# Context attention in the first loop of a fused decoder: values with channels on partitions, denominators from a ones pattern, inverses spread by TensorE

## What is computed

```python
# linear attention, 8 heads of 32
q = x @ Wq + bq; k = x @ Wk + bk; v = x @ Wv + bv
Q = elu(q) + 1; K = elu(k) + 1
KV = einsum('nshd,nshv->nhdv', K, v / L)
Z = 1 / (einsum('nlhd,nhd->nlh', Q, K.sum(axis=1)) + EPS)
x = layernorm(x + einsum('nlhd,nhdv,nlh->nlhv', Q, KV, Z) * L)

# context attention, 16 heads of 16, 64 keys
q = (x @ Wq.T + bq); k = (ctx @ Wk.T + bk); v = (ctx @ Wv.T + bv)
scores = einsum('bqhd,bkhd->bhqk', q, k) / sqrt(16)
attn = softmax(scores)
out = einsum('bhqk,bkhd->bqhd', attn, v)
x = layernorm(x + out @ Wo.T + bo)
```

## Time and profile before

| | before |
|---|---|
| median of three runs | 1464.83 us (1463.44 to 1469.69) |
| profiled execution | 1464.9 us, span 1463.1 us |
| TensorE busy | 88% of the span |
| VectorE busy | 71% |
| ScalarE busy | 35% |
| GpSimd busy | 19% |
| TensorE on the chain that ended last | 75% of the span |
| last normalized rows of loop one | 398.2 us into the span |

### The profile page before, as it was taken

How to read it: one execution, slowest core, us unless ns; L and a number is a source line. 1 busy time by engine, 2 the same in 40 slices (tenths; PEclk the granted TensorE clock), 3 DMA queues, 4 the chain that set the end, 5 groups by cost and what they waited for, 6 DMA issues and landing times.

```text
span 1463.1 us, 17935 instructions
## 1 busy us (share of the span) xinstructions
PE 1287.1 (88%) x7132; PEld 877.9 (60%) x7132; DVE 1037.6 (71%) x1974; ACT 517.5 (35%) x602; POOL 277.1 (19%) x188
## 2 busy tenths in 40 slices
PE   7899999997789999856467999999999999998964
PEld 4566777765644454323345586776867686766653
DVE  4678888885344579967635487887879797878684
ACT  2333333332224567677211233222332323241310
POOL 0111111111000000027100041413223041414141
PEclk9999999996689999978688999999999999999997
DMA  4000000000152045499431202111111000000000
GB/s 191 15 15 30 30 29 15 30 15 0 58 217 101 29 152 192 131 327 325 153 110 41 92 3 68 42 55 55 51 48 62 30 22 19 27 24 28 0 15 15
DMA packets 47059, 104.66 MB, mean 72 GB/s; under 512 B 10496, under 2 KB 31104, under 8 KB 43648
## 3 DMA queue, kind: packets, MB, share of 16 engines
q1 hardware_dynamic: 42816, 101.42, 19.7%
q10 hardware_dynamic: 4160, 2.10, 0.5%
HBM read 59.47 MB, written 44.04 MB: 71 GB/s over the span
## 4 chain that ended last, share of the span: by engine, by line
PE 75%; DVE 13%; ACT 6%; issue 3%; DMA 1%; POOL 1%; SPq 0%; POOLq 0%; DVEq 0%; ACTq 0%
PE ps L1147 7%; PE ps L1207 7%; PE ps L1036 6%; PE ps L872 6%; PE ps L923 5%; PE ps L809 5%; PE ps L716 4%; PE ps L1180 3%; PE ps L1094 2%; PE ps L825 2%; PE ps L789 2%; PE ps L1118 2%; PE ps L1129 2%; PE ps L1224 2%; PE ps L1027 2%
## 5 line engine op out<-in xcount | busy, mean ns | idle before, releaser
L1207 PE MATMUL ps<-arena 128*128 128x256 f32 x512 | 119.8, 388 | 6.7 <-ACT arena L1603 6.7
L1630 POOL TENSOR_TENSOR arena<-arena 128x4 f32<-128x4 f32 x48 | 49.2, 1025 | 369.8 <-DVE arena L1790 369.8
L1147 PE MATMUL ps<-arena 128*128 128x512 f32 x256 | 117.6, 598 | 0.0
L1207 PEld LDWEIGHTS ps<-arena 128*128 128x128 f32 x512 | 98.4, 194 | 28.0 <-ACT arena L1603 10.2
L1036 PE MATMUL ps<-arena 128*128 128x256 f32 x384 | 89.5, 393 | 22.4 <-DVE arena L2051 20.2
L2096 DVE TENSOR_TENSOR arena<-ps,arena 128x2048 f32<-128x2048 f32 x32 | 73.3, 2292 | 39.4 <-PE ps L1094 39.1
L1694 POOL TENSOR_TENSOR arena<-arena 128x16 f32<-128x16 f32 x32 | 92.1, 2913 | 34.1 <-DVE arena L2125 34.1
L1036 PEld LDWEIGHTS ps<-arena 128*128 128x128 f32 x384 | 75.0, 198 | 33.7 <-issue 20.6
L872 PE MATMUL ps<-arena 128*128 128x512 f32 x192 | 85.3, 601 | 1.2 <-ACT arena L1322 1.2
L923 PE MATMUL ps<-arena 128*128 128x512 f32 x192 | 85.0, 595 | 1.4 <-ACT arena L1348 1.4
L809 PEld LDWEIGHTS ps<-arena 128*128 128x128 f32 x512 | 66.4, 209 | 17.9 <-ACT arena L1295 15.3
(11 more groups left out here) (246 smaller groups left out, 2649.9 us busy)
## 6 DMA issues: line engine op xcount, KB each, us to landing
v_scratch<-arena SPq DMA_DIRECT2D x7, 1536.0 KB, 8.5
arena<-v_scratch SPq DMA_DIRECT2D x7, 1536.0 KB, 6.7
up_scratch<-arena SPq DMA_DIRECT2D x6, 1536.0 KB, 7.3
arena<-up_scratch SPq DMA_DIRECT2D x6, 1536.0 KB, 9.4
arena<-x_scratch SPq DMA_DIRECT2D x16, 512.0 KB, 3.9
vw_scratch<-arena SPq DMA_DIRECT2D x32, 256.0 KB, 4.7
arena<-vw_scratch SPq DMA_DIRECT2D x8, 1024.0 KB
arena<-x SPq DMA_DIRECT2D x8, 512.0 KB, 4.2
```

The costliest lines, as they stand in the source:

```text
L1147: last = mm(flat(p % 2), w["cos_wq"][:, k, p * P:(p + 1) * P], xt4[:, k], start=k == 0, stop=k == NC - 1)
L1207: last = mm(flat(2)[:, C:2 * C], cos_pt[:, p], cos_vw[:, par, p], start=p == 0, stop=p == NP - 1)
L1630: g.tensor_tensor(var[0], var[1], neghalf[:, 0:NT], ALU.pow)\
```

## The change

The probabilities of a whole batch are kept: `xat_pt` has room for four tiles. For the values the sides are swapped: the block of values of a pair of heads (128 keys by 32 channels, without ones) is the weights, and the probabilities of that pair for all 512 rows are the moving side, eight products a batch, into four strips of 32 partitions of banks 6 and 7 (`xat_values`). The output thus lies with channels on partitions, as the projection wants it, so the turning of the output and its copy go. The sums come from `xat_denominators`: 32 products with a table of ones and zeros (`sums`, 46 columns, of which a window of 32 slides with tile and pair) as weights, which lay all sums of a batch on 128 partitions by 128 columns of bank 3. One reciprocal inverts them (`xat_reciprocals`). `xat_spread` multiplies the inverses by a second table (`spread`, 2x4x128 columns), so that each channel's partition gets its head's inverse, for all rows, in banks 0 and 1; ScalarE copies that (`xat_copy_spread`), and VectorE multiplies values by it once a batch (`xat_scale`). The output projection goes to banks 2 and 3. The order of the steps on every engine is new, and with it what each step waits for. The two packs that are read only at the start share room with `xat_pt`.

```diff
-            ("blk32", (P,))]
+            ("blk32", (P,)), ("sums", (46,)), ("spread", (NC, NT, P))]
...
-        vbd = ar.take(B, NP, 2 * HD + 2)
+        vbd = ar.take(B, NP, 2 * HD)
...
-        xat_pt = ar.take(NP, P)
-        xat_rec = ar.take(H)
-        xat_o = ar.take(NT, C)
+        probs_at = ar.at
+        xat_pt = ar.take(NT, NP, P)
+        probs_end = ar.at
+        xat_inv = ar.take(P)
+        xat_bc = ar.take(NC, T)
...
-            def xat_values(t):
...
-            def xat_turn_o(b, par):
...
+            def pair_at(c, j):
+
+                return j // 2 * 4 + c * 2 + j % 2
+
+            def xat_denominators(b, par):
+                wait(pe, "xat_probs_copied", b, NT, NT)
+                wait_ahead(pe, "lin_q_biased", b, 2, 1, 1)
+                wait_ahead(pe, "lin_scaled", b, 1, 2, 4)
+                wait_behind(pe, "xat_out_added", b, 1, 1, 1)
+                for t in range(NT):
+                    for c in range(NC):
+                        at = 14 - 4 * t - 2 * c
+                        for j in range(4):
+                            last = mm(flat(3)[32 * j:32 * j + 32, 0:P], w["sums"][:, at:at + 32],
+                                      xat_pt[:, t, pair_at(c, j)], start=t == c == 0,
+                                      stop=t == NT - 1 and c == NC - 1, skip_group_check=True)
+                last.then_inc(sig("xat_den_done").sem, 1)
+
+            def xat_values(b, par):
+                wait(pe, "xat_probs_copied", b, NT, NT)
...
+                for c in range(NC):
+                    for j in range(4):
+                        last = mm(flat(6 + c)[32 * j:32 * j + 32].rearrange("p (t n) -> p t n", t=NT),
+                                  vbd[:, b.off, 4 * c + j], xat_pt[:, :, pair_at(c, j)], start=True, stop=True)
+                last.then_inc(sig("xat_weighted").sem, 1)
+
+            def xat_spread(b, par):
+                wait(pe, "xat_inverted", b)
...
                 for c in range(NC):
                     for t in range(NT):
+                        last = mm(flat(c)[:, t * P:(t + 1) * P], w["spread"][:, c, t], xat_inv, start=True, stop=True)
+                last.then_inc(sig("xat_spread_done").sem, 1)
...
             unrolled(pe, [
...
+                (2, lin_out(1)), (2, lin_out(2)), (3, xat_turn_probs(2)), (2, lin_out(3)), (1, lin_project_kv(0)),
+                (1, lin_project_kv(1)), (1, lin_project_q(0)), (1, lin_project_q(1)), (3, xat_turn_probs(3)),
+                (1, lin_project_kv(2)), (3, xat_denominators), (2, lin_turn_y), (1, lin_project_kv(3)),
+                (2, xat_project_q), (3, xat_spread), (2, xat_scores(0)), (3, xat_values), (2, xat_scores(1)),
+                (3, xat_project_o), (2, xat_turn_probs(0)), (0, lin_turn_x), (2, xat_scores(2)), (1, lin_state),
+                (2, xat_turn_probs(1)), (2, xat_scores(3)), (1, lin_out(0))])
...
             unrolled(act, [
...
+                (3, xat_copy_probs(2)), (3, xat_exp(3)), (1, lin_bias_q), (3, xat_copy_probs(3)), (2, lin_copy_y),
+                (1, lin_exp_k), (2, xat_bias_q), (1, lin_exp_q), (3, xat_copy_spread), (2, xat_exp(0)),
+                (0, lin_copy_x), (2, xat_exp(1)), (2, xat_copy_probs(0)), (2, xat_copy_probs(1)), (2, xat_exp(2))])
...
             unrolled(pool, [
-                (3, rstd("xat", (xat_rs, xat_rs))), (2, xat_residual), (1, lin_add),
-                (1, rstd("lin", (lin_rs, lin_rs)))])
+                (0, lin_add), (0, rstd("lin", (lin_rs, lin_rs))), (2, rstd("xat", (xat_rs, xat_rs))),
+                (1, xat_residual)])
...
+            def xat_reciprocals(b, par):
+                wait(dve, "xat_den_done", b)
+                wait_previous(dve, "xat_spread_done", b)
+                v.reciprocal(xat_inv, flat(3)[:, 0:P]).then_inc(sig("xat_inverted").sem, 1)
+
+            def xat_scale(b, par):
+                wait(dve, "xat_weighted", b)
+                wait(dve, "xat_spread_copied", b)
+                wait_previous(dve, "xat_out_projected", b)
+                v.tensor_tensor(xat_ot.rearrange("p a b -> p (a b)"), flat(6, 2),
+                                xat_bc.rearrange("p a b -> p (a b)"), ALU.mult)\
+                    .then_inc(sig("xat_o_copied").sem, 1)
...
             unrolled(dve, [
...
+                (2, xat_shift(3)), (1, lin_stats), (0, lin_bias_kv(0)), (0, lin_bias_kv(1)), (1, lin_finish),
+                (3, xat_finish), (0, lin_bias_kv(2)), (0, lin_q_negative), (2, xat_reciprocals),
+                (0, lin_bias_kv(3)), (0, lin_k_negative), (2, quantize_part), (0, lin_k_features),
+                (1, xat_shift(0)), (2, xat_scale), (0, lin_q_features), (1, xat_shift(1)), (2, xat_add),
+                (1, xat_shift(2)), (0, lin_mask_state), (3, xat_peak), (0, lin_scale(0)), (0, lin_scale(1)),
+                (0, lin_scale(2)), (0, lin_scale(3))])
```

More of the change, by code:

```diff
@@ L268, in decoder @@
         w.update(w4)
[L269 to L271 removed]
+        assert ar.at <= probs_end
         ar.at = weights
@@ L735, in step @@
                         wait(pe, "lin_q_ready", b)
-                        wait_next(pe, "lin_x_copied", b)
-                    if LIN_BANKS[t] == 3 and not b.first():
-                        pe.wait_ge(sig("xat_normed", NT).sem, sig("xat_normed", NT).at(b, -1))
+                    if t == 0:
+                        wait_ahead(pe, "lin_x_copied", b, 1, 1, 1)
+                        wait_behind(pe, "xat_spread_copied", b, 2, 1, 1)
+                    if t == 1:
+                        wait(pe, "lin_q_biased", b)
+                        wait_behind(pe, "xat_out_added", b, 2, 1, 1)
+                    if t == 2:
+                        wait_ahead(pe, "lin_x_copied", b, 1, 1, 1)
+                        wait_behind(pe, "xat_spread_copied", b, 2, 1, 1)
+                    if t == 3:
+                        wait(pe, "lin_kv_ready", b)
                     for c in range(NC):
@@ L792, in xat_turn_probs @@
                 return step
-            def xat_values(t):
-                def step(b, par):
-                    wait(pe, "xat_probs_copied", b, t + 1, NT)
-                    if t == 0:
-                        if b.first():
-                            pe.wait_ge(ev("vbd_ready"), 1)
-                        wait_previous(pe, "xat_normed", b, NT)
-                        wait_next(pe, "lin_q_biased", b)
-                    else:
-                        wait(pe, "xat_normed", b, t, NT)
-                    if t == NT - 1:
-                        wait_next(pe, "lin_scaled", b, LIN_BANKS.index(3) + 1, NT)
-                    for n in range(NP):
-                        p = n // 2 % 2 * 4 + n // 4 * 2 + n % 2
-                        last = mm(flat(3)[:, p * 34:p * 34 + 34], xat_pt[:, n], vbd[:, b.off, p],
-                                  start=True, stop=True)
-                    last.then_inc(sig("xat_weighted", NT).sem, 1)
-                return step
```

146 lines of the change are left out of this document (76 added, 70 removed).

## The result

The changed kernel takes 1441.76 us (median of four runs, 1441.59 to 1443.83) against 1464.13 for the kernel before beside it. The ratio is 0.984, with a 95% interval from 0.982 to 0.986, so it is faster by 22 us. The profiled execution has a span of 1439.4 us, 23.7 less than before. The last normalized rows of loop one are ready at 372.15 + 1.39 = 373.5 us, where they were at 398.2: 24.7 us are won in loop one, and 1 us is given back behind it.

A forecast was written before the change was run, and what follows sets the result against it. TensorE was taken to set loop one's frame, 38.2 us against 40.7. 302 us plus 68 for the last two batches ends the loop at 370, before 398.2; 1464.9 - 27 = 1438 us, range 1425 to 1452.

The forecast's parts named there:

- Terms of TensorE: TensorE work per loop-one batch: 8.1 us removed, 5.6 us added (denominators 2.0, values 1.76, spreading 1.78), net 2.5 less.
- rival 4: TensorE, loop one: strips don't run side by side for these operands; frame 48 us, total 1490; chance 0.05.
- Change of form: TensorE going between column strips and full array: about 0.15 us at a turning, 0.3 us a frame counted.
- rival 3: TensorE, loop one: each strip/full-array switch costs a full drain, up to 1 us a frame more; 1446; chance 0.08.
- The reciprocal: VectorE, once a batch: inverting 128 elements a partition takes 0.95 us, bounds 0.45 to 1.2.
- The frame: One turn of all loop-one steps, four batches deep: 38.2 us, between 37.4 and 38.8, against 40.7.
- the walk: Step-by-step timing of a new loop-one frame: waits of 0.9, 0.15 and 0.35 us, together 1.4.
- Rival 1: Loop one: hand-offs between VectorE and TensorE bind; frame about 40 us, total 1449; chance 0.14.
- The double frames: Two loop-one frames with a double share of weight rounding on VectorE: shift starts 1.5 us later, 2 x 1.5 us.
- The start: Beginning of loop one: no gain; first full frame at about 71 us, its output projection at 98, before 86.5.
- The drain: Loop one's last two batches: 57 us at full clock, 74 at the lower, 68 taken.
- rival 2: Loop one's last two batches: the clock holds, so they take 57 instead of 68 us; total 1427; chance 0.12.

The follow-up runs named there:

- the run with the early turning: Changed kernel with the newest batch's x turned between the values and second scores, its copy before the first exponential: 1437.2 us.

## Why the prediction was right, point by point

Forecast 1438 us, range 1425 to 1452; measured 1441.8. By the steps:

**Terms of TensorE.** Denominators 2.0 forecast, 1.89 measured; values 1.76, and 1.93 with the 0.17 us by which a group runs on; spreading 1.78, 1.87. The rows of the other loop carried over to within 0.1 us. Their place side by side in four strips (rival 4) was decided by the same rows, and the run on the full array shows the price of being wrong for the values: 4.7 us a frame. (In rival 4 the sum reads 8 x 7 = 58; it is 8 x 7.3, from 48 - 40.7. Nothing else uses it.)

**Change of form.** The turning between two groups in strips was expected to lose 0.15 us; the turning behind the denominators takes 210.19 - 209.26 = 0.93 us for 0.88, so 0.05, and the group of keys and values ahead of them takes 1.81 us (205.56 to 207.37) for 1.72, so 0.09. Around the values no loss shows: the scores ahead of them take 1.07 us as elsewhere. That is about 0.15 us a frame, half of the 0.3 set aside. The Trainium skill (TensorEngine Tiling, Key Properties) has a drain at each such change; the trace shows a loss of 0.05 to 0.09 us at a change here, so rival 3 (up to 1 us a frame) is out.

**VectorE.** The reciprocal was put at 0.95 us from two short ones, and takes that:

```profile
169.20 0.95 DVE L1927 RECIPROCAL arena<-ps 128x128 f32<-128x128 f32 x1
```

**The frame.** The sum gave 37.4 to 38.8, the forecast took 38.2, and it is 37.68. The one wait that the walk found large, 0.9 us at the second scores, is there with 0.72; of the smaller ones the 0.35 us in front of the second turning is there with about 0.2 (the state's products take 2.07 us from start to start for 1.89), and the 0.15 us in front of the projection with less than 0.1. The exchanged steps give 2.4 of the 3.0 us, and the stretched output products, which the forecast had named as old waiting, most of the rest. Rival 1 (hand-overs bind, a frame of about 40) is out.

**The double frames** are the term that was mis-sized: 2 x 1.5 us were forecast, and 39.14 + 40.81 + 39.36 - 3 x 37.68 = 6.3 us came. The late shift was right (2.18 - 0.72 = 1.5 us). What was missed is the clock: TensorE waits 2.18 us there, the granted clock is 0.67 over the projection behind it, part of it at 1.2 GHz, and the projection costs 1.7 us more. The forecast had weighed the clock for the drain alone.

**The start.** The first projection was forecast at 98 us and came at 102.8 in the profile, and at 99.0 in the second profile of the same code. The chain was right; the profile had one stretch at the lower level (0.50 between 40 and 46 us) that I hadn't counted and that not every execution has.

**The drain.** From the first frame of the last two batches 68 us were taken; from 308.06 to 373.5 it is 65.5. The clock was 0.91 and 0.80 there, better than the 0.72 and 0.61 before: rival 2 by a part. Inside it the parts were off by more. The last projection was forecast near 355 us and came at 363.7, 55.6 us into the drain for 53, and behind it the forecast left 15 us where 9.9 were needed.

**The sum.** Together: 4.7 us more from the start, 1.4 more from the frames up to 308.06 (3.3 more in the double frames, less in the full ones), and 2.5 less in the drain make 373.5 us for the 370 forecast; the rest behind the loop gave back 1 us, as set aside. So the mechanism was right, and the total is as near as it is partly because the misses have both signs. The start's 4.7 us stand in one profile of this code and are 1.0 in the other; what lies behind the loop took 1065.9 us in one and 1073.1 in the other.

## What to carry to other kernels

Swapping sides so that the long dimension moves paid here only because the short weights could stand in strips side by side; without them this change would have been slower than what it replaced. Where TensorE nearly fills the frame, a wait costs about its length (1.15 us, and a frame of 39.1 for 37.8, in the run with the early turning), but it can cost nearly twice that through the clock of the group behind it (2.18 us, and 1.7 more in the projection), in most executions though not in all. So put extra work of the engine that it waits for into the drain, or into a place that has slack already. And the order tuned for one set of steps did not hold another here: count on making it anew with the work. Look at a pipelined loop's start and end as well as its frame: here the frames' gain went into a longer start, and the drain brought the rest.

## What was unexpected of the hardware

TensorE fell to its lower level while it was never idle: 64 records with 128x128 weights and only 32 columns each, in one stretch, took 10.9 us instead of 7.2 (7.8 to 10.9 in the first six batches), and full-width groups behind them ran at half speed. As two groups of 16 and one of 32, the same records took 6.9 us. A reciprocal on VectorE takes 0.95 us for 128 elements a partition, 7.4 ns each with its start.

The same file, run twice, had the fall of the clock in its first batch's state product in one profile (3.81 us) and not in the other (2.05 us), and the part behind loop one, the same code in all of these kernels, took from 1065 to 1073 us in the profiles. A single profile's total is no measure of an edit worth a few microseconds.
